# Cross-attention and state scan on one core: row maxima stored to DRAM value by value, with a ones row of minus one

## What is computed

```python
x = _layernorm(builder_state, g1, beta1)          # 4096 x 512
base_n = _layernorm(base_state, g1, beta1)        # 3202 x 512, the context
q, k, v = heads(x, Wq, bq), heads(base_n, Wk, bk), heads(base_n, Wv, bv)   # 8 heads of 64
scores = einsum('bhqd,bhkd->bhqk', q, k) / sqrt(64)
attn = softmax(scores, axis=-1)
out = einsum('bhqk,bhkd->bhqd', attn, v)
x = builder_state + out @ W_o.T + b_o
xn = _layernorm(x, g2, beta2)
U = (xn @ W_in.T + b_in) @ Bmat
s = silu(s @ A.T) + u_t                           # a scan over the 4096 rows
result = x + states @ Cmat + (program_probs.mean(axis=1) @ W_prog.T + b_prog)
```

## Time and profile before

| what | value |
|---|---|
| median of three runs | 2277.15 us |
| time of the profiled execution | 2276.32 us |
| its span | 2274.5 us |
| PE, DVE, POOL, ACT busy | 98%, 75%, 70%, 48% of the span |
| PE's granted clock | 0.995 of full speed |
| DMA packets | 165947, of them 24401 under 512 B |

### The profile page before, as it was taken

How to read it: one execution, slowest core, us unless ns; L and a number is a source line. 1 busy time by engine, 2 the same in 40 slices (tenths; PEclk the granted TensorE clock), 3 DMA queues, 4 the chain that set the end, 5 groups by cost and what they waited for, 6 DMA issues and landing times.

```text
span 2274.5 us, 36100 instructions
## 1 busy us (share of the span) xinstructions
PE 2226.2 (98%) x14168; PEld 1289.4 (57%) x14168; DVE 1711.4 (75%) x2084; ACT 1092.2 (48%) x1416; POOL 1585.3 (70%) x1038
## 2 busy tenths in 40 slices
PE   8999999999999999999999999999999999999987
PEld 8998865455555555555555555555555555445764
DVE  5766646888888888888888888888888888854666
ACT  3654424545444444444444444444544444553454
POOL 1200017888888888888888888888888888988322
PEclk9999999999999999999999999999999999999999
DMA  6660216777767777777777777777777777778734
GB/s 244 204 195 28 75 66 139 155 160 159 157 157 159 161 169 165 170 170 169 166 160 158 170 170 172 169 172 170 161 159 158 164 165 172 169 182 186 232 120 148
DMA packets 165947, 365.42 MB, mean 161 GB/s; under 512 B 24401, under 2 KB 70865, under 8 KB 165266
## 3 DMA queue, kind: packets, MB, share of 16 engines
q0 software_dynamic: 59904, 218.13, 46.9%
q1 hardware_dynamic: 105874, 144.99, 20.0%
HBM read 95.80 MB, written 49.02 MB: 64 GB/s over the span
## 4 chain that ended last, share of the span: by engine, by line
PE 94%; DVE 2%; ACT 2%; DMA 1%; issue 1%; POOL 0%; SPq 0%; DVEq 0%; ACTq 0%; POOLq 0%
PE ps L1429 34%; PE ps L1295 12%; PE ps L1408 8%; PE ps L1406 8%; PE ps L1410 8%; PE ps L1398 5%; PE ps L1258 4%; PE ps L1276 3%; PE ps L1266 3%; PE ps L1496 2%; PE ps L1239 1%; PE ps L1439 1%; PE ps L1248 1%; PE ps L1300 1%; PE ps L1519 1%
## 5 line engine op out<-in xcount | busy, mean ns | idle before, releaser
L772 ACT ACTIVATE pt<-ps 128x1024 f32<-128x1024 f32 x800 | 777.6, 1021 | 889.3 <-PE ps L1410 882.4
L972 DVE TENSOR_REDUCE mx_part<-ps 128x2 f32<-128x1024 f32 x768 | 937.9, 1221 | 337.6 <-PE ps L1295 337.6
L583 POOL TENSOR_TENSOR accp<-accp,pt 128x1024 f32<-128x1024 f32 x416 | 1034.5, 2487 | 208.3 <-ACT pt L772 201.5
L1429 PE MATMUL ps<-pt,v 128*64 128x512 f32 x3328 | 805.6, 605 | 0.0
L1056 DVE TENSOR_TENSOR ps<-ps,shb 128x1024 f32<-128x1024 f32 x403 | 493.2, 1224 | 47.9 <-PE ps L1410 47.9
L1429 PEld LDWEIGHTS ps<-pt,v 128*64 128x64 f32 x3328 | 201.8, 136 | 345.5 <-issue 339.4
L1295 PE MATMUL ps<-kk,qh 64*128 64x512 f32 x1520 | 344.4, 449 | 1.6 <-DVE mx_part L972 1.6
L1295 PEld LDWEIGHTS ps<-kk,qh 64*128 64x128 f32 x1520 | 141.6, 183 | 340.7 <-DVE mx_part L972 250.0
L1406 PE MATMUL ps<-qh,kk 64*128 64x512 f32 x1664 | 327.4, 389 | 2.0 <-ACT pt L772 1.5
L1408 PE MATMUL ps<-qh,kk 64*128 64x512 f32 x1664 | 328.5, 390 | 0.0
L1410 PE MATMUL ps<-ql,kk 64*128 64x512 f32 x1664 | 328.0, 389 | 0.0
(11 more groups left out here) (160 smaller groups left out, 1836.4 us busy)
## 6 DMA issues: line engine op xcount, KB each, us to landing
acca<-pt POOLq DMA_DIRECT2D x224, 512.0 KB, 5.0
accb<-pt POOLq DMA_DIRECT2D x160, 512.0 KB, 4.7
q_scratch<-kk SPq DMA_DIRECT2D x32, 512.0 KB, 4.4
acca<-accp POOLq DMA_DIRECT2D x32, 512.0 KB, 4.6
o_scratch<-ost SPq DMA_DIRECT2D x32, 512.0 KB, 3.0
og<-o_scratch SPq DMA_DIRECT2D x32, 512.0 KB, 5.7
shb<-m_scratch SPq DMA_DIRECT2D x31, 512.0 KB, 4.5
xs<-x SPq DMA_DIRECT2D x16, 512.0 KB, 6.5
```

The source lines that it names most:

```text
L583: nc.gpsimd.tensor_tensor(acc[:, :], acc[:, :], pt[n % PT_SLOTS][:, :], ALU.add).then_inc(added_p, 1)
L772: nc.scalar.activation(pt[n % PT_SLOTS][:, :], src, ACT.Exp, scale=SCALE).then_inc(exped, 1)
L972: nc.vector.tensor_reduce(mx_part[w % 2][:, m % QT, :, m // QT], ps[:, b:b + 2, :], AX_X, ALU.max)\
L1429: ins = mm(ps[HD * h:HD * (h + 1), 6, :], v[:, t, f:f + HD], pt[n % PT_SLOTS][:, h * QB:(h + 1) * QB], start=(t == 0), stop=(t == NT - 1))
```

## The change

`mx_row` gets the type that its readers need (fp32r) and is stored to DRAM straight from its 128 partitions, with the destination indexed so that value (row k, head h, query tile q) lands at position h, 128 q + k. `turn_max` on PE and `shift` on ACT go, with their semaphores and waits. `send_shift` now waits for `max_ready`. The sign that ACT's copy applied is carried by the row of minus ones on PE, and by a subtraction instead of an addition on DVE. `row_max` now waits for the store before it, and `spread_sum` for `den_taken` of the unit before, in place of the semaphores that are gone.

```diff
-TURN_STEP = NJ - M_LEAD
...
-def turn_bank(w):
-
-    return 7 if w else 0
...
-        mx_row = at("mx_row", [P, 2, QT], RR + 11776)
+        mx_row = at("mx_row", [P, 2, QT], RR + 11776, F32R)
...
-        shift_row = at("shift_row", [2 * QT, P], RR + 11840, F32R)
...
             def send_shift(w):
-                sp.wait_ge(shift_ready, w + 1)
+                sp.wait_ge(max_ready, w + 1)
                 wait(sp, sh_loaded, 16 * (w - 1))
                 wait(sp, shb_loaded, 16 * (w - 2))
-                sp.dma_start(m_scratch[w % 2].rearrange("h (q k) -> (h q) k", k=P), shift_row[:, :].bitcast(F32)).then_inc(sh_stored, 16)
+                sp.dma_start(m_scratch[w % 2].rearrange("h (q k) -> k h q", k=P), mx_row[:, :, :].bitcast(F32),
+                             allow_slow_non_contiguous=True).then_inc(sh_stored, 16)
...
-            nc.gpsimd.memset(ones_row[0:1, :].bitcast(F32), 1.0)
-            nc.gpsimd.memset(ones_row[HD:HD + 1, :].bitcast(F32), 1.0).then_inc(ones_set, 1)
+            nc.gpsimd.memset(ones_row[0:1, :].bitcast(F32), -1.0)
+            nc.gpsimd.memset(ones_row[HD:HD + 1, :].bitcast(F32), -1.0).then_inc(ones_set, 1)
...
-            def shift(w):
-                act.wait_ge(max_turned, w + 1)
-                wait(act, sh_stored, 16 * w)
-                nc.scalar.activation(shift_row[:, :], ps[0:2 * QT, turn_bank(w), 0:P], ACT.Copy, scale=-1.0)\
-                    .then_inc(shift_ready, 1)
...
-            shift(0)
...
-                    if j == TURN_STEP and u + 1 < UNITS:
-                        shift(u + 1)
...
             def row_max(w):
                 dve.wait_ge(max_taken, NM * (w + 1) if w else M_EARLY)
-                wait(dve, max_turned, w)
+                wait(dve, sh_stored, 16 * w)
...
-                nc.vector.tensor_tensor(ps[:, b:b + 2, :], ps[:, b:b + 2, :], shb[u % 2][:, :, :], ALU.add)\
+                nc.vector.tensor_tensor(ps[:, b:b + 2, :], ps[:, b:b + 2, :], shb[u % 2][:, :, :], ALU.subtract)\
                     .then_inc(shifted, 1)
...
-            def turn_max(w):
-
-                pe.wait_ge(max_ready, w + 1)
-                wait(pe, den_taken, w - 1)
-                if w == 0:
-                    pe.wait_ge(n_ready, 2 * NG)
-                nc.tensor.transpose(ps[0:2 * QT, turn_bank(w), 0:P], mx_row[:, :, :].rearrange("p h q -> p (h q)"), ident[:, :])\
-                    .then_inc(max_turned, 1)
...
-            turn_max(0)
             project_v(NG - 1, 1)
             pe.wait_ge(k_ready, FC * C_G)
-            pe.wait_ge(shift_ready, 1)
...
                 pe.wait_ge(added_a[u % 2], 16 * (len(A_TILES) + 1) * (u // 2 + 1))
-                if u + 1 < UNITS:
-                    pe.wait_ge(shift_ready, u + 2)
+                wait(pe, den_taken, u)
...
-                    if ahead and j == TURN_STEP:
-                        turn_max(u + 1)
```

More of the change, by code:

```diff
@@ L333, in build @@
         max_done = sem("max_done"); max_taken = sem("max_taken"); max_ready = sem("max_ready")
-        max_turned = sem("max_turned"); shift_ready = sem("shift_ready"); qx_loaded = sem("qx_loaded"); sh_loaded = sem("sh_loaded")
+        qx_loaded = sem("qx_loaded"); sh_loaded = sem("sh_loaded")
         scored = sem("scored"); sh_stored = sem("sh_stored"); shb_loaded = sem("shb_loaded")
```

## The result

The kernel after takes 2287.36 us (2283.88 to 2289.85 in four runs) against 2277.26 us: a ratio of 1.0044, with a 95% interval of 1.0032 to 1.0056. It is 10.1 us slower, where 12.3 us less was forecast. The profiled execution took 2283.88 us, the fastest of the four, with a span of 2282.1 us.

A forecast was written before the change was run, and what follows sets the result against it. PE was taken to bound the kernel: 12.1 us for 31 transposes plus 0.2 us ahead of unit 0, 12.3 us less than the profiled 2276.32, gives 2264.0, or 2264.9 us as median; range 2263.0 to 2271.0 us.

The forecast's parts named there:

- What bounds the kernel, and what leaves PE: In the attention PE bounds; removing 31 transposes at 0.39 us each (0.34 to 0.41) saves 12.1 us.
- the start: Ahead of unit 0, without transpose and ACT's copy, PE's awaited `take_v` starts about 0.2 us sooner, at most 0.3.
- The margin of DVE's loop with PE: PE's second maximum needs DVE's first reduction, which would end 0.11 us before PE gets there; this just fits.
- ACT, DVE and the changed waits: Dropped ACT copies, DVE's subtraction and fp32r reduction, and the new waits on semaphores were all taken as worth nothing.
- S: Time from the issue of the store on SP to its landing: 2.6 us taken, 8.2 us at most.
- the slack: In 31 units the store may take 12 us to land before PE or DVE waits for the shift.
- Unit 0: Store may take only 4.9 us there; nothing late at 2.6 us, one PE wait of 3.3 us at 8.2.
- Traffic beside it: Small packets on the DMA engines shared with POOL's accumulating DMAs: taken as nothing, a few microseconds at the far end.
- The 5 us of room in the buffers: Time left between landing of POOL's accumulating DMAs (5.2 us) and ACT needing the buffer back, three steps after its exponential.
- rival 2: Small packets delay POOL's accumulating DMAs, ACT waits for a buffer; half a microsecond per unit gives 2280 us; chance 0.07.
- The rival with the chance of 0.06 for slower: Store too slow: PE and DVE wait for the shift at each unit's start; 2327 us at 16 us landing; chance 0.06.
- The Trainium skill's factor of 19: Page's slowdown for transposing by rearranged access pattern; by it the store takes 37 us, shift late in every unit.

The follow-up runs named there:

- run 5: Kernel after with its store in 128 pieces of 32 B and the turn left out, so shifts reach wrong query rows: 2266.37 us, ratio 0.9956.
- run 2: Kernel before plus an extra, unread store of the 1024 maxima by value, placed 64 B apart in DRAM: 2277.39 us, ratio 1.0000.
- run 6: Kernel after with only the store ahead of unit 0 in 128 pieces of 32 B, that shift left unturned: 2276.78 us, ratio 1.0003.
- run 1: Kernel before, transpose kept, plus an extra, unread store of the maxima by value in the change's packed layout: 2300.53 us, ratio 1.0101.

## Why the prediction was wrong

**What bounds the kernel, and what leaves PE: right.** The transpose was taken at 0.39 us, and all of it at 12.3 us with the start. Run 5 has 0.36 us in one step, within the bounds of 0.34 to 0.41, and 11.1 us in all. The margin of DVE's loop with PE was enough.

**ACT, DVE and the changed waits: right.** None of them shows in run 5.

**S, the first of two steps that failed.** I took 2.6 us with an upper end of 8.2. In the units SP waits 10.3 us for the store on average and 12.0 at the longest, behind an issue of 0.38 us; so S is 10.7 us. The engines' time for the small packets was rightly priced (the 32768 packets add 0.6% of the engines). But even 64 B apart the values land after 4.0 us (run 2), and packed after 10.9: what was missing is the cost of values that different partitions write side by side. The row that I reasoned from, 32 B pieces, has nothing of this. In the units 12 us were still within the slack: no unit but the first waits for `sh`, and none for `shb`. So in the units S alone cost nothing.

**Unit 0.** I had its slack, 4.9 us, and at worst a wait of 3.3 us. The wait was 3.65 us in the profile. S was 8.4 us there; less the slack of 4.9 us this is 3.5 us, so the slack was right and S was not. The term left out is the lower clock after such a wait, 3.4 us by the windows. Together they are 7 us, against 6.3 us at the start of unit 1 and 10.6 us by the medians of run 6; the difference is not explained.

**Traffic beside it, taken as nothing: the second step that failed.** I counted the engines' time for the small packets, not that a stuck write holds back the packets of other queues. The 5 us of room in the buffers were used up by transfers that landed after 10 us. Run 6 less run 5 is 10.4 us for 31 units, a third of a microsecond each on average. It is not even: the median unit of the kernel after is 54.5 us long, as in run 5 (54.4), and nine units are 0.3 to 4.2 us longer. My rival 2 had this place and half a microsecond, and its sign came true: ACT's waits for `acca` went from 3 to 32. I gave it a chance of 0.07 and no part in the chance for slower.

The sum: 11.1 us less for PE (run 5), 10.4 more in the units and 10.6 more for unit 0 make 9.9 us more; measured are 10.1. This must come out, since the terms are the differences from one median to the next (before, run 5, run 6, after), so it proves nothing. A sum that could have failed is the store alone (run 1) and the gain alone (run 5): 23.1 - 11.1 = 12.0 us against 10.1, apart by no more than the intervals of these runs. The rival with the chance of 0.06 for slower was the late shift in every unit. It did not happen. Two smaller costs did, which I had not added to each other: that is where the chance for slower was too small.

**The Trainium skill's factor of 19** for a transpose by access pattern ("DMA: Bandwidth & Descriptors", Rules for kernel authors) would have had the store at 37 us. It was 10.7, over 5 times the 1.93 us of before. The page's factor is against the hardware's own transpose during a DMA, which the kernel before doesn't use, so the estimate of 37 us had a wrong base. The warning pointed the right way, but run 2 moves as many values by the same kind of pattern in 4.0 us.

## What to carry to other kernels

A store that scatters values of a few bytes should not put the values of many partitions side by side in DRAM: here 8 B of distance made such a store free beside the kernel before, and with a target in SBUF it stalled nothing either. Its price is not in its own packets; look at how long the other queues' transfers take, and at the first time that the chain runs, where the slack is smallest and a stall of PE also costs clock. A freed microsecond on the bounding engine was worth what the starts said; the risk lay in the transfer that took the work over.

## What the runs showed of the hardware that I had not expected

- 1024 writes of 4 B into 4 KB of DRAM land after 10.9 us when each 64 B takes values of 16 partitions, 7.0 us when it takes those of 2 (as two stores of 512), and 5.4, 4.4 and 4.0 us at distances of 8, 16 and 64 B.
- While the packed ones are pending, nearly nothing of another queue lands for about 4 us (0 to 82 GB/s instead of 165), and its packets take up to 5.6 us.
- PE idle for 3.65 us was followed by windows of 6 us with a granted clock of 0.69 and 0.74.
- A stride of 16 B in SBUF made PE's 512-column fp32r product 618 instead of 394 ns; a stride of 32 B made DVE's subtraction over 128 x 1024 2068 instead of 1224 ns.

What stays open: why the step lies between 4 and 8 B, and whether it is the number of DMA engines in one piece of DRAM or the number of partitions. Nothing here tells the two apart. Open is also how the loss is shared between unit 0 and the others, where medians and traces disagree by 3 to 4 us.
